# Token loads inside two attention projections, later waits at the cosine stage, and the context's high part behind the keys' in an eight-stage kernel

## The chip, the cores and the metric

The kernel runs on one core of one Trainium2 chip, as one program of 83187 instructions. The metric is the device time of one launch in microseconds (us). A core has five engines with queues of their own: PE (matrix products; its weight loads are listed as PEld), DVE (vector), ACT (scalar, activations), POOL (GpSimd) and SP, which here only issues transfers and waits. They order their work among each other by semaphores alone. A `Block` in the code holds one program for each engine and ends with a barrier of all of them.

## The reference, cut to what matters

Eight batches of 512 tokens of 256 numbers (4096 tokens, 4 MB) go through four layers. Each layer adds an attention over the context and then a feed-forward part:

```
x = x + attention0(context, layernorm(x), mask);     x = x + top-1 experts(layernorm(x))
x = x + cosine attention(layernorm(x), context);     x = x + expert choice(layernorm(x))
x = x + attention2(layernorm(x), context);           x = x + piecewise linear ffn(layernorm(x))
x = x + attention3(layernorm(x), context, mask);     x = x + top-2 experts(x)
```

Attentions 0, 2 and 3 have 16 heads of 16 numbers: `q = layernorm(x) Wq + bq`, `k = context Wk + bk`, `v = context Wv + bv`, softmax, and an output product. The cosine attention normalises tokens and context (with a gain `ln_g` and an offset `ln_b`), and needs sums over all tokens before it can weigh its three terms. Its weights are `w_in`, `w_out` and `b_out`.

## The kernel before, in words

The tokens are resident on the chip in `G.X`, 128 partitions x 32 tiles x 256 numbers. `build_program` fills constants in a first block, in which SP also stores a block of blank rows and loads the eight batches of tokens (L3312 to L3314, one semaphore `x_loaded[b]` for each). The eight stages follow one another, each of them blocks of its own.

**Projections** (`resident_projections`, L1353) are the first block of attentions 0, 2 and 3. Each product is made of three, from a high and a low part of both operands. Order by engine, for the batch b of the loop:

- SP loads the weights and the contexts of batches 0 and 1, five small tensors, for attention 0 also a mask; then in each round the context of b + 2 (it waits for `cT_low`), the stores of the key parts and of the query parts (four each), and what `prepare.loads` asks for: from round 4 on twelve loads of a group of heads (fourteen in attention 3), in attention 0 a mask of 1 MB in rounds 3 and 5.
- ACT: the root for the layernorm of b + 1 (`scalar_roots`), the high part of the context of b + 1 (`context_high`, L1460), the high part of the keys of b, of the queries of b (`high_part`, L1471), of the turned tokens of b + 1 (L230).
- POOL: the low part of the context of b (L1493), then what `prepare.gpsimd` asks for: in rounds 0 and 1 two fills each of `a_qs` or `a_ks` with ones (L1641); in attention 0 in rounds 2 to 7 conversions of the masks.
- DVE: the layernorm of b + 1 (statistics L200, aggregation L205, `a_p_var` L208, reciprocal L210, four `a_p_xn` L215), the low part of the keys of b (L1507), the values (L1528), the low part of the queries, of the turned tokens of b + 1 (L221).
- PE: keys, values, queries of b (24 products each, the 24 of the values half as wide), then eight transposes of `a_p_xn` of b + 1. Keys of b + 1 need the context's low part and free `psK` (`k_low`).

Key and query parts are held in one buffer in attention 0 and in two in the others. The profile writes `a_` for the prefixes of all three attentions.

**Cosine attention** (`cosine_attention`, L2046) first loads `win`, `wout` and `bout` in a block of their own with `load_weights` (L76), which waits until they have landed. `cosine_sums` (L2068) then loads `lng` and `lnb` the same way, sets two constants in a third block, and in a fourth goes over the batches: SP loads the context `cx`, DVE normalises, POOL applies gain and offset (L2177, L2178), PE turns and sums. `win` is first read in the next function, `wout` and `bout` in the one after.

**Expert choice** (`expert_choice`, L2700) uses the room of `G.X` for expert weights and keeps the tokens in DRAM (`x_dram`). At its end a block loads all 4 MB back and waits for them (L2711 to L2713). Attention 2 is the next stage.

Of the kernel before, what the change touches and what calls it, by code (L numbers as in the profile page):

```python
# [14 lines left out]
P = 128  # L15
B = 8
# [3 lines left out]
TB = S // P  # L20
# [1332 lines left out]
def resident_projections(nc, A, G, nm, w, q_scale, q_dram, k_dram, V, wo, bo, buffers, prepare):  # L1353

    with ExitStack() as ctx:
# [22 lines left out]
        rows = lambda x: x.rearrange("(k p) d -> p k d", p=P)  # L1378

        with nc.Block() as block:  # L1380
            @block.sync
            def _(sp):
                def context(b):
                    sp.dma_start(cT[:, b % 2], ctxT[:, :, b * S:(b + 1) * S]).then_inc(cT_loaded[b % 2], 16)

                sp.dma_start(raw["wk"][:], rows(w.Wk)).then_inc(w_loaded["wk"], 16)
                context(0)
                sp.dma_start(raw["wv"][:], rows(w.Wv)).then_inc(w_loaded["wv"], 16)
                sp.dma_start(raw["wq"][:], rows(w.Wq)).then_inc(w_loaded["wq"], 16)
                context(1)  # L1390
                smalls = ((bk[:], w.bk), (bv[:], bcast_row(w.bv)), (bq[:], w.bq), (wo[:], rows(w.Wo)), (bo[:], bcast_row(w.bo)))
                for tile, src in smalls:
# [10 lines left out]
                for b in range(B):  # L1403
                    if b + 2 < B:
                        sp.wait_ge(cT_low, b + 1)
                        context(b + 2)
                    sp.wait_ge(k_low, b + 1)
                    store(kp[:, b % buffers], k_dram[:, b], k_stored[b % buffers])
                    sp.wait_ge(q_low, b + 1)
                    store(qp[:, b % buffers], q_dram[:, b], q_stored[b % buffers])  # L1410
                    if b == 4:
                        for stored in k_stored + q_stored:
                            sp.wait_ge(stored, 64 * b // buffers)
                    prepare.loads(sp, b)
# [40 lines left out]
            def _(act):  # L1455
# [24 lines left out]
                for b in range(B):  # L1480
                    if b + 1 < B:
                        f.scalar_roots(act, b + 1)
                        context_high(b + 1)
                    high_part(k_in_psum, psK, kp, bk, k_stored, k_high, b)
                    high_part(q_in_psum, psQ, qp, bqs, q_stored, q_high, b)
                    if b + 1 < B:
                        f.scalar_high(act, b + 1, 0)
# [10 lines left out]
            def _(dve):  # L1498
# [11 lines left out]

                dve.wait_ge(G.x_loaded[0], 16)
                f.vector_norm(dve, 0, 0, first=True)
# [9 lines left out]
                for b in range(B):  # L1522
                    if b + 1 < B:
                        dve.wait_ge(G.x_loaded[b + 1], 16)
                        f.vector_norm(dve, b + 1, b + 1)
# [520 lines left out]
def cosine_attention(nc, A, G):  # L2046
# [4 lines left out]
    with ExitStack() as ctx:  # L2051
# [3 lines left out]
        bout = sb("bout", [P, D])  # L2055
# [3 lines left out]
        loaded = sem("loaded")  # L2059
        load_weights(nc, [(win[:], A["L1_xattn_w_in"].rearrange("(k p) o -> p k o", p=P)),  # L2060
                          (wout[:], A["L1_xattn_w_out"].rearrange("(h p) d -> p h d", p=P)),
                          (bout[:], bcast_row(A["L1_xattn_b_out"]))], loaded)
        cosine_sums(nc, A, G, z_dram, gsum)
        cosine_weights(nc, A, G, win, gsum, coef, wwh)
        cosine_apply(nc, A, G, z_dram, win, wout, bout, coef, wwh)


def cosine_sums(nc, A, G, z_dram, gsum):  # L2068


    with ExitStack() as ctx:
# [20 lines left out]
        zT_in_psum, zT_ready = [sem("zkT_in_psum"), sem("zqT_in_psum")], [sem("zkT_ready"), sem("zqT_ready")]  # L2092
        load_weights(nc, [(lng[:], bcast_row(A["L1_xattn_ln_g"])), (lnb[:], bcast_row(A["L1_xattn_ln_b"]))], loaded)
        with nc.Block() as block:
# [12 lines left out]
        with nc.Block() as block:  # L2107
            @block.sync
            def _(sp):
                load = lambda b, s: sp.dma_start(cx[:, s], ctx_rows[bass.ds(b, 1)].rearrange("a p t d -> p (a t) d")).then_inc(cx_loaded[s], 16)  # L2110
                load(0, 0)

                def step(b, u, i):
# [9 lines left out]
                for n in range(2):  # L2123
                    sp.wait_ge(z_stored[n], (B + 1) * 16)
                    sp.wait_ge(cx_loaded[n], (B // 2 + 1 - n) * 16)

            @block.tensor
# [41 lines left out]
            def _(pool):  # L2169
                def step(b, u, i):  # L2170
                    link = chained(pool, pool_chain, b * 2)

                    for z, x, ready, done in ((zk, nk, nk_ready, zk_ready), (zq, nq, nq_ready, zq_ready)):
# [4 lines left out]
                        nc.gpsimd.tensor_tensor(z[:, u], z[:, u], o, ALU.add).then_inc(done, 1)  # L2178

                rounds(pool, step)  # L2180

# [518 lines left out]
def expert_choice(nc, A, G):  # L2700
# [6 lines left out]
    with ExitStack() as ctx:  # L2707
        index = ctx.enter_context(nc.sbuf_tensor("l1f_index", [P, CE, SB], U32))
        choose_tokens(nc, A, G, sT_dram, index)
        run_experts(nc, A, G, rows_dram[0:N_TOK, :], x_dram, index)  # L2710
    with ExitStack() as ctx:  # L2711
        back = ctx.enter_context(stage_semaphores(nc, "l1f_"))("back")
        load_weights(nc, [(G.X[:], x_dram.rearrange("(n p) d -> p n d", p=P))], back)  # L2713

# [573 lines left out]
def build_program(nc, A, out, stages):  # L3288
    with ExitStack() as ctx:
# [11 lines left out]
        out_dram = out.rearrange("b s d -> (b s) d").rearrange("(n p) d -> p n d", p=P)  # L3301
        G.x_loaded, G.out = x_loaded, out_dram

        G.blank_rows = nc.dram_tensor("blank_rows", [P, TOP1_ROW], F32).ap()
        G.top1_rows = nc.dram_tensor("top1_rows", [TOP1_BLOCKS * P, TOP1_ROW], F32).ap()
        G.filled, blank_set, blank_stored = sem("filled"), sem("blank_set"), sem("blank_stored")
        with nc.sbuf_tensor("blank", [P, TOP1_ROW], F32) as blank, nc.Block() as block:
            @block.sync
            def _(sp):
                sp.wait_ge(blank_set, 2)  # L3310
                sp.dma_start(G.blank_rows, blank[:]).then_inc(blank_stored, 16)
                for b in range(B):  # L3312
                    sp.dma_start(G.X[:, b * TB:(b + 1) * TB, :], x_dram[:, b * TB:(b + 1) * TB, :]).then_inc(x_loaded[b], 16)
                sp.wait_ge(blank_stored, 16)  # L3314
# [58 lines left out]
```

## Time and profile before

| | us |
|---|---|
| median of three runs | 4579.55 (4572.97 to 4582.59) |
| the profiled execution, its own time | 4560.4 |
| its span | 4558.6 |
| PE busy | 3880.8 (85%) |
| DVE busy | 3103.2 (68%) |
| ACT busy | 2059.7 (45%) |
| POOL busy | 794.4 (17%) |

The span is what lies between the first and the last instruction of the profiled execution. Busy times are shares of that span; engines overlap, so that they don't add up. The span holds long stretches with different limits, and a mean over it says little of any one of them. Times in the rows below are counted from the span's start. Attention 0's projections lie between 10 and 137 us, the cosine attention begins at 1182, attention 2's projections lie between 2884 and 2996, attention 3's between 3743 and 3856.

### The profile page before, as it was taken

The numbers are of one execution on the slowest core, as the hardware profiler recorded it, in microseconds if no ns is written. First come the engines' busy times: TensorE is split into PE (matmuls) and PEld (weight loads), VectorE is DVE, ScalarE is ACT, GpSimd is POOL, SyncE is SP. The second block draws the span as 40 slices with busy tenths as digits, with TensorE's granted clock in tenths as the row PEclk, the third lists the DMA queues.
The fourth block names the chain that finished last, engine by engine and source line by source line (L and its number), as shares of the span: only waits on it lengthen the run. The fifth ranks groups of instructions, "written<-read, shape, count | busy, mean of one in ns | idle before, by whom it ended". The sixth has DMA issues, their size and how long they took to land. (4 is left out here: it accounts for less than half of the span.)

```text
span 4558.6 us, 83187 instructions
## 1 busy us (share of the span) xinstructions
PE 3880.8 (85%) x30525; PEld 2807.5 (62%) x30525; DVE 3103.2 (68%) x7110; ACT 2059.7 (45%) x3636; POOL 794.4 (17%) x510
## 2 busy tenths in 40 slices
PE   6699997799367999786389999579997987999899
PEld 5344444798265777676378888445555665455577
DVE  7666664446656666544556666678876888988688
ACT  3255554134013333243044444247775763777511
POOL 5424321401341000000023322310000003000000
PEclk9799998599678999898599999779998998999999
DMA  7333321201321000011054444532210005122000
GB/s 248 102 99 99 99 90 52 70 25 43 112 75 33 14 18 18 28 44 37 6 159 125 128 130 124 188 112 66 66 44 19 1 26 207 56 67 67 30 19 19
DMA packets 234365, 338.02 MB, mean 74 GB/s; under 512 B 39092, under 2 KB 132837, under 8 KB 234054
## 3 DMA queue, kind: packets, MB, share of 16 engines
q1 hardware_dynamic: 218168, 306.66, 21.1%
q0 software_dynamic: 15888, 27.23, 2.9%
q8 instruction: 195, 3.19, 0.3%
q14 instruction: 114, 0.93, 0.1%
HBM read 242.42 MB, written 107.01 MB: 77 GB/s over the span
## 5 line engine op out<-in xcount | busy, mean ns | idle before, releaser
L1905 ACT ACTIVATE a_pT<-a_psS 128x512 f32<-128x512 f32 x1536 | 835.9, 598 | 380.4 <-PE a_psS L1791 375.0
L1977 DVE TENSOR_REDUCE a_mx<-a_psA 128x1 f32<-128x512 f32 x1024 | 656.4, 685 | 77.4 <-PE a_psA L1769 77.4
L1806 PE MATMUL a_psZ<-a_pT,a_V 128*17 128x128 f32 x12288 | 485.8, 277 | 0.0
L1769 PE MATMUL a_psA<-a_ks,a_qs 48*128 48x512 f32 (+1 forms) x1536 | 402.8, 520 | 85.1 <-DVE a_mx L1977 36.8
L1973 DVE CUSTOM_DVE_ANT_0 a_scored<-a_psA,a_hide_q 128x512 bf16<-128x512 f32 x512 | 332.6, 688 | 182.1 <-PE a_psA L1769 181.0
L1806 PEld LDWEIGHTS a_psZ<-a_pT,a_V 128*17 128x17 f32 x12288 | 272.0, 97 | 269.4 <-issue 152.4
L1769 PEld LDWEIGHTS a_psA<-a_ks,a_qs 48*128 48x128 f32 (+1 forms) x1536 | 150.9, 191 | 331.4 <-DVE a_mx L1977 124.8
L1791 PE MATMUL a_psS<-a_qs,a_ks 50*128 50x512 f32 (+1 forms) x1536 | 316.3, 405 | 2.7 <-ACT a_pT L1905 0.8
L3245 DVE SCALAR_TENSOR_TENSOR ex_h<-ex_psU,ex_ub,ex_sg 128x512 f32<-128x512 f32 x129 | 96.9, 751 | 189.4 <-PE ex_psU L159 182.3
L1989 POOL TENSOR_TENSOR X<-X,a_osb 128x512 f32<-128x512 f32 x48 | 61.1, 1278 | 931.3 <-ACT a_osb L1892 913.3
L3191 ACT CAST ex_w_h<-X 128x1024 fp32r<-128x1024 f32 x102 | 106.0, 1040 | 151.0 <-DMA X<-in_L_ffn_gw 147.2
L1779 PE MATMUL a_psS<-a_hide_k,identb 128*128 128x512 bf16 x512 | 154.9, 384 | 16.5 <-ACT a_pT L1905 2.9
L3200 ACT ACTIVATE ex_sg<-ex_psG,ex_gb 128x512 f32<-128x512 f32 x129 | 88.8, 688 | 169.0 <-PE ex_psG L159 168.9
L3112 POOL DMA_INDIRECT ex_xg<-l1f_rows,ex_idx_get x72 | 75.4, 1047 | 511.5 <-DVEq L3276 361.8
L1791 PEld LDWEIGHTS a_psS<-a_qs,a_ks 50*128 50x128 f32 (+1 forms) x1536 | 148.5, 188 | 18.2 <-ACT a_pT L1905 13.1
L159 PE MATMUL ex_psY<-ex_w_h,ex_h_l 128*128 128x256 f32 x512 | 143.7, 281 | 0.0
L158 PE MATMUL ex_psY<-ex_w_l,ex_h_h 128*128 128x256 f32 x512 | 143.5, 280 | 0.0
L157 PE MATMUL ex_psY<-ex_w_h,ex_h_h 128*128 128x256 f32 x512 | 143.5, 280 | 0.0
L1148 PE MATMUL p_psY<-p_w,p_h 128*128 128x256 f32 x512 | 131.4, 392 | 13.5 <-ACT p_h L1225 13.5
L157 PE MATMUL l1a_psF<-l1a_win_h,l1a_zh 128*128 128x512 f32 x288 | 120.5, 418 | 25.4 <-DVE l1a_zl L2603 12.0
L1493 POOL TENSOR_TENSOR a_p_cT_l<-a_p_cT,a_p_cT_h 128x1024 fp32r<-128x1024 f32 x24 | 58.6, 2441 | 455.9 <-ACT a_p_cT_h L1460 455.4
L3205 ACT CAST ex_h_h<-ex_h 128x512 fp32r<-128x512 f32 x129 | 80.3, 623 | 116.7 <-DVE ex_h L3245 116.7
(606 smaller groups left out, 10221.8 us busy)
## 6 DMA issues: line engine op xcount, KB each, us to landing
a_qs<-a_q_parts SPq DMA_DIRECT2D x576, 64.0 KB, 2.3
a_ks<-a_k_parts SPq DMA_DIRECT2D x576, 64.0 KB, 2.3
a_k_parts<-a_p_kp SPq DMA_DIRECT2D x96, 256.0 KB, 2.6
a_q_parts<-a_p_qp SPq DMA_DIRECT2D x96, 256.0 KB, 3.1
X<-in_L_ffn_gw SPq DMA_DIRECT2D x36, 512.0 KB, 4.5
X<-in_L_ffn_up_w SPq DMA_DIRECT2D x36, 512.0 KB, 3.3
X<-in_L_ffn_down_w SPq DMA_DIRECT2D x36, 512.0 KB, 3.9
top_rows<-blank_rows SPq DMA_DIRECT2D x32, 514.0 KB, 5.0
```

The lines of the kernel that those rows point to most:

```text
L157: nc.tensor.matmul(out, wh, xh, start=start and n == 0, stop=False, **kw)
L158: nc.tensor.matmul(out, wh, xl, start=False, stop=False, **kw)
L159: last = nc.tensor.matmul(out, wl, xh, start=False, stop=stop and n == len(pairs) - 1, **kw)
L1148: last = nc.tensor.matmul(out, h[:, m % 2, t * P:(t + 1) * P], w2[:, m, :], start=False, stop=(m == MF - 1), skip_group_check=True)
L1769: nc.tensor.matmul(psA[:, unit(a, par) % 3], qs[r, g % ring, p % 2, q * P:(q + 1) * P], ks[r, g % ring, p % 2], start=True, stop=True).the ...
L1779: nc.tensor.matmul(psS[:, unit(t, par) % 3], G.identb[:], hide_k[:, u % 2, kt, :], start=True, stop=False, skip_group_check=True)
L1791: nc.tensor.matmul(psS[:, unit(t, par) % 3], ks[r, g % ring, p % 2, kt * P:(kt + 1) * P], qs[r, g % ring, p % 2], start=(hidden is None), ...
L1806: last = nc.tensor.matmul(psZ[q * VP:q * VP + VW, g % 2, j * P:(j + 1) * P], V[:, b, kt, g % NG * GH + j, :], pT[:, p % 2, par, kt, q * P: ...
L1905: nc.scalar.activation(pT[:, p % 2, par, kt, :], psS[:, unit(t, par) % 3], ACT.Exp).then_inc(exp_done, 1)
L1973: nc.vector.tensor_tensor_reduce(out=scored[:, par], in0=psA[:, unit(a, par) % 3], in1=hide_q[:, b % 2, q, :], scale=1.0, scalar=HIDDEN, o ...
L1977: nc.vector.tensor_reduce(mx[:, p // 2 % 2, par, p % 2, q:q + 1], psA[:, unit(a, par) % 3], AX_X, ALU.max).then_inc(a_used, 1)
L3191: nc.scalar.copy(w_h[:, s, c, :], whole[:, c, :]).then_inc(w_high, 1)
```

## The change

Four edits:

- The first block doesn't load the tokens any more. Attention 0's projections take them from `G.x_from`, batch by batch: batch 0 ahead of all weights, batch 1 after the context of batch 1, batch b + 2 at the head of round b.
- Expert choice doesn't load the tokens back. It leaves the place in DRAM in `G.x_from`, and attention 2's projections load them in the same way. `G.x_loads` counts the stages that did so, for the semaphore's value. Attention 3 has none to load.
- The cosine attention issues all five weight loads behind the load of the first context, in the block that goes over the batches. Only POOL waits for `lng` and `lnb`, ahead of its first round; SP waits for all of them at the block's end. Two blocks with waits are gone.
- In all three projections ACT makes the high part of the keys of b ahead of the high part of the context of b + 1.

```diff
@@ resident_projections
+        x_from, G.x_from = G.x_from, None
+        G.x_loads += x_from is not None
...
+                def tokens(b):
+                    if x_from is not None:
+                        tiles = slice(b * TB, (b + 1) * TB)
+                        sp.dma_start(G.X[:, tiles, :], x_from[:, tiles, :]).then_inc(G.x_loaded[b], 16)
...
+                tokens(0)
                 sp.dma_start(raw["wk"][:], rows(w.Wk)).then_inc(w_loaded["wk"], 16)
                 context(0)
                 sp.dma_start(raw["wv"][:], rows(w.Wv)).then_inc(w_loaded["wv"], 16)
                 sp.dma_start(raw["wq"][:], rows(w.Wq)).then_inc(w_loaded["wq"], 16)
                 context(1)
+                tokens(1)
...
                     if b + 2 < B:
+                        tokens(b + 2)
                         sp.wait_ge(cT_low, b + 1)
                         context(b + 2)
...
                         f.scalar_roots(act, b + 1)
+                    high_part(k_in_psum, psK, kp, bk, k_stored, k_high, b)
+                    if b + 1 < B:
                         context_high(b + 1)
-                    high_part(k_in_psum, psK, kp, bk, k_stored, k_high, b)
                     high_part(q_in_psum, psQ, qp, bqs, q_stored, q_high, b)
...
-                dve.wait_ge(G.x_loaded[0], 16)
+                dve.wait_ge(G.x_loaded[0], 16 * G.x_loads)
...
-                        dve.wait_ge(G.x_loaded[b + 1], 16)
+                        dve.wait_ge(G.x_loaded[b + 1], 16 * G.x_loads)
@@ cosine_attention
-        load_weights(nc, [(win[:], A["L1_xattn_w_in"].rearrange("(k p) o -> p k o", p=P)),
-                          (wout[:], A["L1_xattn_w_out"].rearrange("(h p) d -> p h d", p=P)),
-                          (bout[:], bcast_row(A["L1_xattn_b_out"]))], loaded)
-        cosine_sums(nc, A, G, z_dram, gsum)
+        loads = [(win[:], A["L1_xattn_w_in"].rearrange("(k p) o -> p k o", p=P)),
+                 (wout[:], A["L1_xattn_w_out"].rearrange("(h p) d -> p h d", p=P)),
+                 (bout[:], bcast_row(A["L1_xattn_b_out"]))]
+        cosine_sums(nc, A, G, z_dram, gsum, loads, loaded)
@@ cosine_sums
-        load_weights(nc, [(lng[:], bcast_row(A["L1_xattn_ln_g"])), (lnb[:], bcast_row(A["L1_xattn_ln_b"]))], loaded)
...
                 load(0, 0)
+                for tile, src in ((lng, "L1_xattn_ln_g"), (lnb, "L1_xattn_ln_b")):
+                    sp.dma_start(tile[:], bcast_row(A[src])).then_inc(loaded, 16)
+                for tile, src in later_loads:
+                    sp.dma_start(tile, src).then_inc(later_loaded, 16)
...
+                sp.wait_ge(loaded, 32)
+                sp.wait_ge(later_loaded, 16 * len(later_loads))
...
+                pool.wait_ge(loaded, 32)
                 rounds(pool, step)
@@ expert_choice
-    with ExitStack() as ctx:
-        back = ctx.enter_context(stage_semaphores(nc, "l1f_"))("back")
-        load_weights(nc, [(G.X[:], x_dram.rearrange("(n p) d -> p n d", p=P))], back)
+    G.x_from = x_dram.rearrange("(n p) d -> p n d", p=P)
@@ build_program
+        G.x_from, G.x_loads = x_dram, 0
...
-                for b in range(B):
-                    sp.dma_start(G.X[:, b * TB:(b + 1) * TB, :], x_dram[:, b * TB:(b + 1) * TB, :]).then_inc(x_loaded[b], 16)
```

## Rows read from the trace of the kernel before

**Rows 1.** Windows by stage: engines' busy us (count), granted clock, DMA share, GB/s.

```profile
10.00:23.00 13.00, 1.97 (x8) 1.53 (x8) 5.40 (x17) 5.12 (x7) 2.05 (x1) 1.00 1.09 361
...
1182.00:1197.00 15.00, 0.00 (x0) 0.00 (x0) 0.17 (x2) 0.00 (x0) 0.00 (x0) 0.50 0.55 166
...
2862.00:2884.00 22.00, 0.00 (x0) 0.00 (x0) 0.11 (x1) 0.15 (x1) 0.00 (x0) 0.50 0.64 197
...
2930.00:2941.00 11.00, 9.73 (x56) 8.20 (x56) 10.51 (x22) 4.67 (x9) 2.48 (x1) 1.00 0.67 240
```

**Rows 2.** Timeline, kernel's start: start us, us, engine, line, output<-input, count.

```profile
1.60 8.56 SPq L3313 DMA_DIRECT2D X<-in_x  x8
...
10.61 1.48 SPq L1386 DMA_DIRECT2D a_p_wk_raw<-in_L_xattn_Wk  x1
...
19.82 1.04 ACT L1460 CAST a_p_cT_h<-a_p_cT 128x1024 fp32r<-128x1024 f32 x1 [0.68 <-DMA a_p_cT<-in_ctxT]
```

**Rows 3.** DMA issues between 0 and 40 us: count, KB each, us to landing.

```profile
blank_rows<-blank SPq DMA_DIRECT2D x1, 128.5 KB, 3.3
```

**Rows 4.** Timeline, entry of the cosine attention.

```profile
1182.34 0.38 SPq L82 DMA_DIRECT2D l_win<-in_L_xattn_w_in  x1
...
1196.60 0.17 DVE L2097 MEMSET l1s_zeros<- 128x128 f32 x1 [16.63 <-PEq L78]
...
1197.25 1.19 SPq L2110 DMA_DIRECT2D l1s_cx<-in_ctx  x2
...
1201.20 1.41 DVE L2192 BATCH_NORM_STATS2 l1s_stats<-X 128x6 f32 x4 [4.43 <-DMA l1s_cx<-in_ctx]
```

**Rows 5.** Timeline, from the experts' end into attention 2, SP and ACT.

```profile
2869.03 0.39 SPq L82 DMA_DIRECT2D X<-l1f_x  x1
2883.84 0.39 SPq L1386 DMA_DIRECT2D a_p_wk_raw<-in_L_xattn_Wk  x1
...
2889.57 1.04 ACT L1460 CAST a_p_cT_h<-a_p_cT 128x1024 fp32r<-128x1024 f32 x1 [2.28 <-DMA a_p_cT<-in_ctxT]
```

**Rows 6.** DMA issues between 2920 and 2970 us.

```profile
a_p_cT<-in_ctxT SPq DMA_DIRECT2D x4, 512.0 KB, 4.3
```

**Rows 7.** Timeline of attention 2's round 2, by engine (ACT, POOL, DVE).

```profile
2925.59 0.21 ACT L226 ACTIVATE a_p_std<-a_p_var 128x4 f32<-128x4 f32 x1 [5.44 <-DVE a_p_var L208]
2925.70 1.03 ACT L1460 CAST a_p_cT_h<-a_p_cT 128x1024 fp32r<-128x1024 f32 x1
2926.64 1.26 ACT L1471 ACTIVATE a_p_kp<-a_p_psK,a_p_bk 128x512 fp32r<-128x512 f32 x2
...
2936.48 0.20 ACT L226 ACTIVATE a_p_std<-a_p_var 128x4 f32<-128x4 f32 x1 [5.44 <-DVE a_p_var L208]
...
2926.88 2.47 POOL L1493 TENSOR_TENSOR a_p_cT_l<-a_p_cT,a_p_cT_h 128x1024 fp32r<-128x1024 f32 x1 [8.42 <-ACT a_p_cT_h L1460]
...
2926.04 3.46 DVE L215 TENSOR_SCALAR a_p_xn<-X,a_p_meanvar,a_p_rstd 128x256 f32<-128x256 f32 x4
```

**Rows 8.** Timeline of DVE in attention 0 while POOL waits for a mask.

```profile
74.83 1.38 DVE L215 TENSOR_SCALAR a_p_xn<-X,a_p_meanvar,a_p_rstd 128x256 f32<-128x256 f32 x4
```

**Rows 9.** Timeline of POOL and DVE, attention 2's round 1; last row attention 0.

```profile
2905.81 8.82 POOL L1641 MEMSET a_ks<- 32x5120 f32 x2
...
2912.68 1.99 DVE L208 TENSOR_SCALAR a_p_var<-a_p_meanvar 128x4 f32<-128x4 f32 x1
...
85.25 10.44 DVE L215 TENSOR_SCALAR a_p_xn<-X,a_p_meanvar,a_p_rstd 128x256 f32<-128x256 f32 x4
```

**Rows 10.** Timeline of SP in attention 2 from the query store of round 4.

```profile
2955.08 2.45 SPq L1401 DMA_DIRECT2D a_q_parts<-a_p_qp  x4
...
2963.57 0.42 SPq L1384 DMA_DIRECT2D a_p_cT<-in_ctxT  x1
...
2989.06 2.68 SPq L1401 DMA_DIRECT2D a_q_parts<-a_p_qp  x4
```

**Rows 11.** Timeline of POOL in attention 0, the first conversion of the second mask.

```profile
79.37 5.38 POOL L1624 TENSOR_SCALAR a_is_hidden<-a_m_int 128x2048 f32<-128x2048 int32 x1 [12.12 <-DMA a_m_int<-in_maskT]
```

More of the change, by code:

```diff
@@ L2059, in cosine_attention, with cosine_sums @@
         loaded = sem("loaded")
-        load_weights(nc, [(win[:], A["L1_xattn_w_in"].rearrange("(k p) o -> p k o", p=P)),
-                          (wout[:], A["L1_xattn_w_out"].rearrange("(h p) d -> p h d", p=P)),
-                          (bout[:], bcast_row(A["L1_xattn_b_out"]))], loaded)
-        cosine_sums(nc, A, G, z_dram, gsum)
+        loads = [(win[:], A["L1_xattn_w_in"].rearrange("(k p) o -> p k o", p=P)),
+                 (wout[:], A["L1_xattn_w_out"].rearrange("(h p) d -> p h d", p=P)),
+                 (bout[:], bcast_row(A["L1_xattn_b_out"]))]
+        cosine_sums(nc, A, G, z_dram, gsum, loads, loaded)
         cosine_weights(nc, A, G, win, gsum, coef, wwh)
         cosine_apply(nc, A, G, z_dram, win, wout, bout, coef, wwh)
-def cosine_sums(nc, A, G, z_dram, gsum):
+def cosine_sums(nc, A, G, z_dram, gsum, later_loads, later_loaded):
     with ExitStack() as ctx:
```

## The prediction

> **What bounds the kernel now.** I read the page's 40 slices first: PE is busy over most of the span, but not everywhere, so a mean can't price this change. Next came windows on the five places it touches. In two of them all engines stand still and only transfers run: 15 us at the cosine attention's entry, 22 us between the experts and attention 2 [rows 1]. Last I read timelines. They show what ends those pauses [rows 4, 5], what ends the wait at the kernel's start [rows 2], and which engine sets a round of the projections. In an undisturbed round of attention 2 the roots stand 2936.48 - 2925.59 = 10.9 us apart [rows 7]; DVE is busy for 10.51 of 11 us, PE for 9.73, ACT for 4.67 [rows 1]. DVE sets the round, and PE's 9.7 is the next floor.
>
> **Part 1, tokens at the kernel's start.** SP spends 8.56 us on issuing eight token loads, and the weights follow at 10.61; the first context's high part, from which the keys follow, starts at 19.82 because its transfer is late [rows 2]. That is 9.2 us after the stage's first load. The same way takes 2889.57 - 2883.84 = 5.7 us in attention 2, with an empty queue [rows 5]. After the change the first block ends once the blank rows have landed: issued just ahead of the token loads, at about 1.2, plus 3.3 [rows 3], plus 0.45 for the barrier (wk follows the last token issue, 1.60 + 8.56 = 10.16, by that much) = 4.95. One token batch (512 KB) now stands ahead of weights and context. At the 361 GB/s that the queue moves while it is full [rows 1] it takes 1.4 us. So the high part starts at 4.95 + 5.7 + 1.4 = 12.05, 7.8 earlier. I take 7.5, with 5 (slow first issues, 1.07 us each in the row of eight) and 8.5 as ends. The layernorm of batch 0 isn't later: tokens landed after some 3.5 us plus 2.2 of statistics come to 5.7, before the context's 7.1.
>
> **Part 2, cosine entry.** Two blocks of loads go. DVE's constants, at 1196.60, move to where SP issued the first load, 1182.34, and the context load follows 0.65 us behind as now (1197.25): at 1183.0, 14.25 earlier [rows 4]. The context needs 3.95 us to land now (1201.20), with one context behind it. Five loads, 2.4 MB, now queue behind it; I allow 0.45 for packets that mix. Sum 13.8, ends 12 and 14.3. Hidden: POOL first needs gain and offset some 7 us after DVE's first statistics, that is 11 us after the issue, and the second context (behind all five, about 9 us) is needed 14 us after the first. If that cover were gone, POOL would start late by the difference, once.
>
> **Part 3, entry of attention 2.** SP's load of all tokens is issued at 2869.03, the stage's first load at 2883.84 [rows 5]. The block between them goes: 14.8 us. The context of batch 0 stands behind one token batch: 1.4 us back. Gain 13.4, ends 10 and 14.8 (nothing given back).
>
> **Part 4, six token loads in the rounds.** In a round SP issues 0.45 us more and the queue moves 0.5 MB more beside 2.6 MB; its share goes from 0.67 [rows 1] to some 0.8. SP waits for DVE there, so the issue is free. The load for batch b + 2 starts behind the query store of b - 1, some 2.3 us after DVE has made it, and DVE reads it 1.1 us plus a round after it: 9.7 + 1.1 - 2.3 = 8.5 us of cover. A context, the same size from the same place in the queue, lands in 4.3 [rows 6]; with 1.4 for the tokens that is 5.7. In rounds 4 to 6 of attention 2 SP issues without a gap from 2955.08 to 2989.06 + 2.68 = 2991.74, and the stage ends behind that. There the load for batch 7 (beside the context at 2963.57) costs its 0.45 [rows 10]. It may also land up to 3 us after DVE wants it, which is hidden: DVE's last results wait for SP then.
>
> **Part 5, the order on ACT.** Four `a_p_xn` take 3.46 us while POOL makes the context's low part (2926.88 to 2929.35), and end when it ends [rows 7]; the same four take 1.38 while POOL is idle [rows 8]. DVE loses 2.08 us a round by this overlap. With the keys' high part first (two instructions, 1.15 us until the next can start) POOL starts about 2.4 us after the root instead of 1.3, and the four end 1.8 after it: no overlap. The keys' high part needs nothing that is late: the root comes some 2 us after the keys' last product. DVE alone would then need 8.8 us a round, PE needs 9.7, and the context's low part, 1.15 later, ends 4.9 us after the root, just when PE wants it. So a round becomes 9.7, a gain of 1.2.
>
> The Trainium skill ("SBUF — State Buffer", on engine ports) says that VectorE's two-port operations and GpSimd share one port pair as an exclusive lock for a whole instruction, first come first served. By that rule four xn cost either 1.38 or what POOL leaves, never a mixture; rows 7 and 8 agree. The rule also speaks against this change where POOL's work is long, which is priced next from rows.
>
> Where POOL has more to do, the shift costs. In round 1 of attentions 2 and 3 it fills a stack with two instructions, 8.82 us [rows 9]. DVE's `a_p_var` waited there to their end (2912.68 + 1.99), and in attention 0 four xn took 10.44 us while POOL ran three instructions back to back, so one DVE instruction gets in between two of POOL's [rows 9]. After the change the fills stand at 2907.0 to 2911.4 to 2915.8. DVE is there 2.1 earlier (2910.6), passes at 2911.4, and its first xn waits until 2915.8, the second behind the context's low part until 2918.3. The keys' low part starts at 2919.0 against 2918.5: 0.4 lost. The next rounds give back 1.9 (DVE has slack over PE there), then 0.4, then 1.2 and a last 0.5 at the query part that SP stores at 2955.08: 3.6 us in each stage. From there SP's issues set the end, so rounds 5 to 7 bring nothing. Attention 3: 3.6. Attention 2: 3.6 - 0.45 = 3.1. Ends for each: -1 (all rounds like round 1) and 7 (1.2 in six rounds).
>
> In attention 0 POOL has 7 us of fills or mask work in rounds 0 to 3, and the root waits for it: up to 1.15 us a round lost, 3.5 in all. But POOL then waits 12.12 us for a mask [rows 11] that SP issues behind the queries of round 3. These come 0.8 to 3 us earlier by my walk through the rounds, depending on whether DVE slips between two fills. I take 1.0, ends -3.5 and 3.
>
> **Sum.** 7.5 + 13.8 + 13.4 + 1.0 + 3.1 + 3.6 = 42.4 us. The profiled execution, 4560.4 (span 4558.6), would become 4518.0. It lies 19 us under the median of the runs shown; against that median, 4579.55, the forecast is **4537 us**.
>
> **Rivals.**
> - *The order on ACT pays back less than it costs*: in each round with POOL work the chain root, keys' high, context's high, low part, POOL's own work grows by 1.15 us, and that chain sets the round: three rounds of attention 0 and two each of attentions 2 and 3, 8 us lost and the 7.7 of part 5 not won. 42.4 - 7.7 - 8 = 27 us gained: 4553. For it: `a_p_var` ends with POOL's fill [rows 9]. Against: undisturbed rounds are set by DVE.
> - *The order pays fully*, 1.2 us in six rounds of each of attentions 2 and 3 and 3 us in attention 0: 34.7 + 3 + 6.7 + 7.2 = 52 gained: 4528. Against: SP's gapless issues from round 4.
> - *The entries were hidden anyway*: the blocks' waits go, but the first context lands as late because the queue is as full. All load bytes still stand in one queue. Then parts 1 to 3 bring half, 17 us, 25 in all: 4555. Against: only one token batch is ahead of what PE needs.
> - *Slower*: token loads arrive late in every round, and DVE, which takes them in order, waits with all behind it (keys' low part, stores, PE). They have 8.5 us of cover. Each us above it costs 12 us (six rounds, two stages); the gain of 42 is gone from 8.5 + 3.5 = 12 us to landing. At 14 us it is +24: 4604. Against: 4.3 for a context in that place [rows 6].
>
> **How the numbers follow.** The forecast with its own ends holds 0.62, the order's loss 0.13, its full pay 0.12, half-hidden entries 0.07, late tokens 0.03 (a part of which ends within the bound), the rest mishaps and the scatter of runs, whose three span 10 us. Range 4519 to 4557: from both good ends (60 gained) down to 22 gained. This kernel's measurement tells some 0.2%, 9 us, from no change. Faster by more: 0.95; within: 0.03; slower: 0.02.
>
> **What would show it.** The high part of context 0 starts near 12 us after the span's start; the cosine context load less than 1 us after the end of the top-1 stage's barrier, with DVE's statistics 4 to 4.5 us behind; the pause before attention 2 shrinks by 13; four xn take 1.4 in rounds 2 to 6, with rounds of 9.7 us in attentions 2 and 3; round 1 longer. Waits of DVE's statistics for X in the rounds, or POOL ahead of the root in them, would prove me wrong. If the DVE stall stays at 2 us a round though POOL starts later, part 5 is wrong.

## The result and the profile after

The changed kernel took 4534.9 us in the median of four runs (4525.88 to 4540.46), the kernel before 4576.69 beside it (4572.97 to 4582.59, four runs). The ratio is 0.9908, 95% interval 0.9892 to 0.9924: 42 us faster. A later set gave 4539.0 (six runs) beside 4574.09, ratio 0.9919, 0.9906 to 0.9932. Forecast: 4537, range 4519 to 4557; it was counted down from 4579.55, the median of the three runs known then. The profiled execution took 4525.88 us.

The page of the changed kernel, first lines:

```profile
span 4524.1 us, 83053 instructions
...
PE 3878.7 (86%) x30431; PEld 2817.1 (62%) x30525; DVE 3076.4 (68%) x7110; ACT 2058.1 (45%) x3636; POOL 794.6 (18%) x510
```

PE's work is as before (3880.8 us). DVE's busy time fell by 27 us with the same work. The `a_p_xn` of all three projections together take 57.8 us, where they took 85.6: what went are stalls that the profile counts as busy. The kernel's start, changed kernel, timeline:

```profile
4.27 0.45 SPq L1390 DMA_DIRECT2D X<-in_x  x1
4.77 0.50 SPq L1396 DMA_DIRECT2D a_p_wk_raw<-in_L_xattn_Wk  x1
...
8.53 1.41 DVE L200 BATCH_NORM_STATS2 a_p_stats<-X 128x6 f32<-128x256 f32 x4 [8.53 <-DMA X<-in_x]
...
11.33 1.03 ACT L1472 CAST a_p_cT_h<-a_p_cT 128x1024 fp32r<-128x1024 f32 x1
```

The stage's first load is issued at 4.27, and the first high part starts at 11.33, not at 19.82 [rows 2]. The entry of the cosine attention, changed kernel, timeline:

```profile
1170.40 1.23 DVE L1044 TENSOR_TENSOR X<-X,m_rows 128x1024 f32<-128x1024 f32 x1 [0.23 <-DMA m_rows<-m_z]
1174.07 0.17 DVE L2109 MEMSET l1s_zeros<- 128x128 f32 x1 [2.44 <-PEq L46]
...
1174.74 0.38 SPq L2122 DMA_DIRECT2D l1s_cx<-in_ctx  x1
1175.17 0.50 SPq L2125 DMA_DIRECT2D l1s_lng<-in_L_xattn_ln_g  x1
...
1178.83 1.41 DVE L2211 BATCH_NORM_STATS2 l1s_stats<-X 128x6 f32 x4 [4.59 <-SPq L2131]
```

Between the barrier and the context's load no other load is waited for, and the statistics come 4.1 us after its issue, nearly as before (3.95) [rows 4]. POOL's first product with the gain comes 7.08 us after the first statistics in both kernels, so POOL doesn't wait for `lng` and `lnb`. The releaser of the last row is given as a wait of SP; the time is that of the load's landing. The entry of attention 2, changed kernel, SP and ACT:

```profile
2848.11 0.39 SPq L1390 DMA_DIRECT2D X<-l1f_x  x1
2848.56 0.50 SPq L1396 DMA_DIRECT2D a_p_wk_raw<-in_L_xattn_Wk  x1
...
2854.83 1.03 ACT L1472 CAST a_p_cT_h<-a_p_cT 128x1024 fp32r<-128x1024 f32 x1
```

The high part starts 6.7 us after the first load of the tokens, where it was 2889.57 - 2869.03 = 20.5 [rows 5]. Rounds 1 and 2 of attention 2, changed kernel, timelines of ACT, POOL and DVE:

```profile
2876.42 0.65 DVE L208 TENSOR_SCALAR a_p_var<-a_p_meanvar 128x4 f32<-128x4 f32 x1
2877.57 7.15 DVE L215 TENSOR_SCALAR a_p_xn<-X,a_p_meanvar,a_p_rstd 128x256 f32<-128x256 f32 x4
...
2892.49 1.38 DVE L215 TENSOR_SCALAR a_p_xn<-X,a_p_meanvar,a_p_rstd 128x256 f32<-128x256 f32 x4
...
2872.69 8.79 POOL L1654 MEMSET a_ks<- 32x5120 f32 x2
2881.55 2.37 POOL L1506 TENSOR_TENSOR a_p_cT_l<-a_p_cT,a_p_cT_h 128x1024 fp32r<-128x1024 f32 x1
2894.47 2.40 POOL L1506 TENSOR_TENSOR a_p_cT_l<-a_p_cT,a_p_cT_h 128x1024 fp32r<-128x1024 f32 x1 [10.55 <-ACT a_p_cT_h L1472]
...
2892.03 0.20 ACT L226 ACTIVATE a_p_std<-a_p_var 128x4 f32<-128x4 f32 x1 [5.77 <-DVE a_p_var L208]
2901.76 0.20 ACT L226 ACTIVATE a_p_std<-a_p_var 128x4 f32<-128x4 f32 x1 [3.34 <-DVE a_p_var L208]
```

In round 2 the four `a_p_xn` end at 2893.87, before POOL starts at 2894.47: 1.38 us, not 3.46 [rows 7]. In round 1 they stand behind the fill and the low part for 7.15 us: the first takes 4.06 (to the fill's end), the second 2.53 (to the low part's end), the last two 0.40 each. Windows over one undisturbed round of attention 2 and one of attention 3, changed kernel (columns as in [rows 1]):

```profile
2892.03:2901.76 9.73, 9.73 (x62) 8.56 (x61) 8.50 (x20) 4.47 (x8) 2.40 (x1) 1.00 0.88 311
3767.20:3777.00 9.80, 9.80 (x62) 8.71 (x61) 8.51 (x20) 4.47 (x7) 2.40 (x1) 1.00 0.79 285
```

PE is busy all of the round: it has taken DVE's place as what sets it. SP's tail of attention 2 and, last, DVE's wait for the tokens of batch 7, changed kernel:

```profile
2917.53 2.75 SPq L1412 DMA_DIRECT2D a_q_parts<-a_p_qp  x4
...
2926.00 0.43 SPq L1390 DMA_DIRECT2D X<-l1f_x  x1
...
2929.55 3.61 SPq L1412 DMA_DIRECT2D a_q_parts<-a_p_qp  x4
...
2952.62 2.79 SPq L1412 DMA_DIRECT2D a_q_parts<-a_p_qp  x4
...
2930.40 1.41 DVE L200 BATCH_NORM_STATS2 a_p_stats<-X 128x6 f32<-128x256 f32 x4 [2.25 <-DMA X<-l1f_x]
```

From the query store of round 4 to the end of the last it is 37.9 us, and 36.7 before (2991.74 - 2955.08) [rows 10]: 0.47 of the token load, the rest slower issues. Attention 0, POOL of the changed kernel:

```profile
70.53 5.38 POOL L1637 TENSOR_SCALAR a_is_hidden<-a_m_int 128x2048 f32<-128x2048 int32 x1 [9.64 <-DMA a_m_int<-in_maskT]
...
100.60 7.09 POOL L1622 TENSOR_SCALAR a_hide_q<-a_m_int 128x2048 bf16<-128x2048 int32 x1 [12.01 <-DMA a_m_int<-in_mask_Bx1xSxS_ik]
```

The wait that was 12.12 us [rows 11] is now 9.64 and ends 8.84 us earlier, about as much as the stage started earlier (8.49). SP's queue shows why, first in the kernel before, then in the changed kernel:

```profile
71.20 1.82 SPq L1401 DMA_DIRECT2D a_q_parts<-a_p_qp  x4
73.06 0.45 SPq L1603 DMA_DIRECT2D a_m_int<-in_maskT  x1
```

```profile
62.37 1.80 SPq L1412 DMA_DIRECT2D a_q_parts<-a_p_qp  x4
64.21 0.46 SPq L1616 DMA_DIRECT2D a_m_int<-in_maskT  x1
```

Counted from the first high part, the queries of round 3 are stored at 51.0 us, where it was 51.4, and the mask's conversion follows its issue by 6.3 us in both. Nothing of the new order came through. The statistics of batch 2 come 1.5 us earlier than before (17.9 for 19.5), those of batch 4 come 0.5 later (42.0 for 41.5), because the two rounds between them take 12.0 us each for 11.0. POOL reached its wait 2.1 us later than before.

### The profile page after: what moved, and what is told of

The parts are those of the page before. It is cut to its first block and busy times, and to the rows that moved or that the text cites. A ratio compares the mean times of both kernels' runs of the same rounds, so it can differ in the third digit from the quotient of the medians.

```text
span 4524.1 us, 83053 instructions
## 1 busy us (share of the span) xinstructions
PE 3878.7 (86%) x30431; PEld 2817.1 (62%) x30525; DVE 3076.4 (68%) x7110; ACT 2058.1 (45%) x3636; POOL 794.6 (18%) x510
## 5 line engine op out<-in xcount | busy, mean ns | idle before, releaser
L1792 PE MATMUL a_psS<-a_hide_k,identb 128*128 128x512 bf16 x418 | 133.8, 383 | 28.0 <-ACT a_pT L1918 15.8
```

The source lines that it names most:

```text
L1792: nc.tensor.matmul(psS[:, unit(t, par) % 3], G.identb[:], hide_k[:, u % 2, kt, :], start=True, stop=False, skip_group_check=True)
```

## The experiments

The table takes the touched stretches alone, from each kernel's profile, in us. *start*: the first context's high part, from the span's start. *a0*: first context's high part to the end of attention 0's projections (DVE's `memset` of `a_nparts`). *cos*: end of the last addition before the cosine attention to its first statistics. *entry*: from the start of DVE's last group on `ex_y` (the experts' result) to attention 2's first high part. *a2*: from there to the query store of round 4, and to the end of the projections. *a3*: first statistics to the same two places. *sh*: the shared expert (part of expert choice), from first to last of its normalizing instructions, whose code no kernel changes.

| kernel | start | a0 | cos | entry | a2 | a3 | sh |
|---|---|---|---|---|---|---|---|
| before | 19.82 | 117.68 | 21.24 | 36.38 | 65.51, 106.95 | 71.41, 113.24 | 196.5 |
| changed | 11.33 | 117.63 | 7.20 | 22.58 | 62.70, 105.11 | 66.58, 109.23 | 196.9 |
| changed, again | 10.75 | 119.45 | 7.10 | 23.07 | 62.34, 104.59 | 66.62, 108.27 | 207.4 |
| old order | 11.06 | 119.16 | 7.27 | 22.90 | 66.10, 109.22 | 69.90, 111.64 | 207.6 |
| cosine only | 19.79 | 122.38 | 7.09 | 35.11 | 65.89, 106.78 | 71.67, 113.81 | 207.5 |
| tokens only | 12.14 | 123.04 | 21.04 | 22.71 | 66.04, 108.27 | 71.84, 114.24 | 196.3 |
| order only | 20.01 | 119.29 | 20.69 | 34.94 | 63.41, 105.55 | 66.89, 109.25 | 196.5 |
| masks earlier | 10.94 | 106.52 | 7.09 | 22.67 | 62.84, 105.78 | 66.54, 108.22 | 200.4 |
| fills spread | 11.00 | 120.27 | 7.11 | 22.71 | 55.24, 97.48 | 59.06, 101.54 | 196.5 |
| both | 10.95 | 107.71 | 7.10 | 22.66 | 55.27, 97.53 | 58.93, 101.78 | 196.3 |
| both, again | 11.55 | 106.09 | 7.08 | 22.59 | 55.24, 97.85 | 59.68, 102.12 | 196.9 |
| tokens first | 22.27 | 119.39 | 7.20 | 32.79 | 62.27, 103.00 | 66.95, 109.19 | 196.6 |
| a round later | 10.72 | 142.80 | 7.05 | 22.60 | 81.07, 140.06 | 67.07, 108.59 | 207.5 |

The runs were made in four sets, not all on one chip, each with the kernel before beside it: its medians are 4576.69, 4573.53, 4572.0 and 4574.09. So where two kernels come from different sets, their distance is also given "by the ratios": the difference of their ratios to the kernel before, times 4574 us. The changed kernel has two ratios, 0.9908 and 0.9919, which gives two ends.

**The change without its new order.** Edit to the changed kernel:

```diff
                         f.scalar_roots(act, b + 1)
+                        context_high(b + 1)
                     high_part(k_in_psum, psK, kp, bk, k_stored, k_high, b)
-                    if b + 1 < B:
-                        context_high(b + 1)
```

> The changed kernel with the old order on ACT (context's high part ahead of the keys'). Theory: the order brought 2 to 3 us in attention 2 and 4 in attention 3 by taking four xn out of POOL's way, and nothing in attention 0, where masks set the end; so this kernel takes 5 to 8 us more than the changed one and about 35 less than the one before. Its xn are 3.46 us again in rounds 2 to 6 and its rounds 10.9 us. Rival (the order costs as much as it brings): same time as the changed kernel within 2 us. Rival (the order is most of the gain): 15 us or more above the changed kernel.

4545.22 us (4532.69 to 4552.47), ratio 0.9939 (0.9916 to 0.9963). The old order costs 109.22 - 105.11 = 4.1 us in attention 2 and 2.4 in attention 3, together within the 5 to 8 expected. The median is 10.3 us above the changed kernel's 4534.9, and 9 to 14 by the ratios; what lies beyond the two stretches isn't explained. Its timeline of DVE in attention 2 has the old stall in rounds 2 and 3, though all else is new:

```profile
2903.23 3.45 DVE L215 TENSOR_SCALAR a_p_xn<-X,a_p_meanvar,a_p_rstd 128x256 f32<-128x256 f32 x4
...
2914.11 3.46 DVE L215 TENSOR_SCALAR a_p_xn<-X,a_p_meanvar,a_p_rstd 128x256 f32<-128x256 f32 x4
```

**Each part alone**, put into the kernel before: the cosine hunks, the token hunks (the block of the start and that of expert choice together), the order.

```diff
# cosine only
-        cosine_sums(nc, A, G, z_dram, gsum)
+        cosine_sums(nc, A, G, z_dram, gsum, loads, loaded)
# tokens only
-        load_weights(nc, [(G.X[:], x_dram.rearrange("(n p) d -> p n d", p=P))], back)
+    G.x_from = x_dram.rearrange("(n p) d -> p n d", p=P)
# order only
+                    high_part(k_in_psum, psK, kp, bk, k_stored, k_high, b)
+                    if b + 1 < B:
                         context_high(b + 1)
-                    high_part(k_in_psum, psK, kp, bk, k_stored, k_high, b)
```

> The kernel before with the cosine attention's loads alone changed. Theory: the stage's first statistics start 14 us earlier and all of it reaches the end: 14 us under the kernel before. Rival (the weights are still waited for later): the gain is under 5 us, and a pause shows ahead of the sums' end or the next function.

> The kernel before with the token loads alone changed, old order on ACT, old cosine entry. Theory: 8.5 us at attention 0's first context and 13.8 at attention 2's, less 0.5 at attention 2's end for the issue of batch 7: 21 to 22 us under the kernel before. In this order a round takes 10.9 us, so batch 7's tokens land less late than in the changed kernel (under 1 us of wait for X). Rival (loads late in every round): DVE waits for X in several rounds and the gain falls under 15.

> The kernel before with the order on ACT alone changed. Theory: attention 0's projections end within 1 us of before; attention 2's end 3 to 4 us earlier relative to their start (no token load stands in SP's gapless issues), attention 3's 4; together 7 us under the kernel before. In round 1 of both, four xn take 7 us. Rival (port contention is not what lengthens xn): xn stay at 3.4 us in rounds 2 to 6 although POOL starts later. Rival (the order loses where POOL has work): slower than before.

Cosine only: 4563.26 (4554.62 to 4570.93, ten runs), ratio 0.9977 (0.9962 to 0.9991). Tokens only: 4550.06 (4547.15 to 4554.33), 0.9958 (0.9942 to 0.9975). Order only: 4568.48 (4559.93 to 4575.96, ten runs), 0.9995 (0.9986 to 1.0005), whose interval holds 1; its stretches tell it from nothing: 1.4 us in attention 2, 4.0 in attention 3. Against the 4573.53 of the kernel before in that set the medians are 10.3, 23.5 and 5.1 lower (14, 21 to 22 and 7 were expected), 38.9 in all; by the ratios they are 10.5, 19.2 and 2.3, 32.0 in all; the whole change brought 42 and 35. The touched stretches say it best: 14.1 at the cosine entry, 7.7 + 13.7 at the two entries, 1.4 + 4.0 in the rounds, 40.9 beside 42.2 for the whole. So within the scatter the parts add up, and nothing shows that one needs another. Attention 0's rest was 5.4 us longer with the tokens alone and 4.7 longer with the cosine hunks alone, which don't touch it: differences of 5 us in that stretch can't be read. With the tokens alone DVE waited 3.27 us for the late `a_bo`, and 0.66 in the kernel before.

The profiled execution of cosine only was 9.2 us longer than that of the kernel before, though its cosine entry is 14.1 us shorter. The stretch *sh* shows where part of that went: cosine only was 10.9 us ahead at its start and 0.1 behind at its end. Another 9 us were lost after it. Windows over it in cosine only, then in the changed kernel:

```profile
1915.80:2123.30 207.50, 179.31 (x983) 156.02 (x984) 86.86 (x188) 84.43 (x117) 0.00 (x0) 0.87 0.13 40
```

```profile
1905.20:2102.10 196.90, 173.43 (x982) 148.59 (x983) 86.85 (x189) 84.40 (x117) 0.00 (x0) 0.92 0.14 43
```

DVE and ACT do the same work in both; PE has the same count of instructions at a mean granted clock of 0.87, not 0.92, and is busy for 6 us more of the 10.6. Four of the thirteen profiled executions of the table (changed again, old order, cosine only, a round later) took some 207.5 us there at 0.86 or 0.87, eight some 196.5 at 0.92, and one 200.4 at 0.90. The changed kernel shows both.

**Masks a round earlier.** Edit to the changed kernel:

```diff
-            if hidden is not None and b in (3, 5):
-                load_mask(sp, (b - 1) // 2)
+            if hidden is not None and b in (2, 4):
+                load_mask(sp, b // 2)
```

> The changed kernel, with the two later masks of attention 0 issued one round earlier (in rounds 2 and 4, not 3 and 5). Theory (attention 0's middle rounds wait for masks, so the new order could bring nothing there): POOL's two waits of 9.6 and 12.0 us for a mask shrink below 2 us each and the stage's end, at 128.96 us in the changed kernel, comes 8 to 14 us earlier; the median is 8 to 14 us under the changed kernel's 4534.9, so 4521 to 4527. Rival (the mask's 4 us issue-side place is taken from the stores, or DVE's own work sets these rounds): the waits go but the end moves by under 3 us, median 4532 to 4538.

4516.87 (4516.02 to 4517.74), ratio 0.9878 (0.9862 to 0.9895). Attention 0's projections are 117.63 - 106.52 = 11.1 us shorter, inside the 8 to 14 expected. The median is 18.0 us under the changed kernel's 4534.9, and 14 to 19 by the ratios, so somewhat more than the stretch explains. Its timelines have one wait of POOL for a mask left, and a new one of DVE, for the tokens of batch 7:

```profile
85.70 7.09 POOL L1622 TENSOR_SCALAR a_hide_q<-a_m_int 128x2048 bf16<-128x2048 int32 x1 [2.27 <-DMA a_m_int<-in_mask_Bx1xSxS_ik]
...
89.60 1.41 DVE L200 BATCH_NORM_STATS2 a_p_stats<-X 128x6 f32<-128x256 f32 x4 [4.26 <-DMA X<-in_x]
```

The masks' landing had set those rounds. With it out of the way the late token load of the last batch is what shows next (3.2 and 4.4 us in the two profiles of *both*).

**Fills spread.** Edit to the changed kernel, for attentions 2 and 3:

```diff
-            if b < 2:
+            if hidden is None and b < 4:
+                half = (32, 96)[b % 2]
+                nc.gpsimd.memset((qs, ks)[b // 2][half:half + 32].bitcast(F32), 1.0).then_inc(stacks_set, 1)
+                pool.wait_ge(stacks_set, b + 1)
+            if hidden is not None and b < 2:
```

> The changed kernel, with the four fills of POOL in attentions 2 and 3 spread one per round over rounds 0 to 3, where they were two in each of rounds 0 and 1. Theory (one DVE instruction slips between two of POOL's, the rest wait for the engine's whole stretch; the order loses in round 1 because a fill and the low part lie back to back beside the four normalizing instructions): in round 1 the slow instruction (7.15 us) goes back to under 3.5 us, and the part up to the query store of round 4 is 4 to 7 us shorter in each of the two stages; median 8 to 14 us under the changed kernel's, 4521 to 4527. Rival (POOL's fill time is on the chain anyway, so that spreading moves the loss to rounds 2 and 3): each of the four rounds loses 4.4 us of POOL in the chain root, fill, low part, and the stages' ends stay within 1.5 us; median 4532 to 4538.

4523.59 (4513.41 to 4526.2), ratio 0.9887 (0.987 to 0.9905). The part up to the query store of round 4 is 7.5 us shorter in both stages (62.70 to 55.24, 66.58 to 59.06), over the 4 to 7 expected; the median is 11.3 us under the changed kernel's, and 10 to 15 by the ratios. Timelines of POOL and DVE in attention 2's round 1, fills spread:

```profile
2872.08 2.40 POOL L1506 TENSOR_TENSOR a_p_cT_l<-a_p_cT,a_p_cT_h 128x1024 fp32r<-128x1024 f32 x1 [4.75 <-ACT a_p_cT_h L1472]
2874.53 4.37 POOL L1654 MEMSET a_qs<- 32x5120 f32 x1
...
2870.08 1.38 DVE L215 TENSOR_SCALAR a_p_xn<-X,a_p_meanvar,a_p_rstd 128x256 f32<-128x256 f32 x4
```

The fill ends at 2878.90, just before DVE's next `a_p_var` at 2879.07, so neither waits for the other; the `a_p_xn` take 1.38 or 1.39 in every round of attention 2, and no stall of DVE on a fill is left there.

**Both.** The two edits together, in two sets of runs.

> Both at once: masks one round earlier in attention 0, fills spread in attentions 2 and 3. By the theories of the two single runs they act in different stages and add up: 16 to 28 us under the changed kernel's median, 4507 to 4519. By the rivals: under 4 us, 4531 to 4539. If only one of the two holds: 4521 to 4527.

> The kernel with the masks of attention 0 one round earlier and the fills of attentions 2 and 3 spread over four rounds, run again in more rounds beside the kernel before. Its first run gave 4500.0. Theory (both edits add up): 4500 +- 8, ratio to the kernel before 0.982 to 0.987. Rival (part of the 35 us below the changed kernel was the scatter of one set of runs): 4512 to 4520, ratio 0.987 to 0.989.

> The changed kernel itself, beside the two others of this set, so that both differences are read on one chip and in one set of runs. Theory: 4535 +- 8, ratio to the kernel before 0.989 to 0.993; stages' steps as in its first profile within 1 us where PE's clock has no part (first context's high part, the cosine attention's statistics, attention 2's first context). Rival (the steps hold by chance): any of these three off by more than 2 us.

First set 4500.04 (4495.18 to 4512.13), ratio to the kernel before 0.9848 (0.9827 to 0.9868); second 4509.07 (4503.24 to 4511.14), 0.9856 (0.9839 to 0.9873), beside the changed kernel's 4539.0 in the same set. That is 30 us below the changed kernel and beats both single edits. The second median lies 1 us outside the expected 4500 +- 8, its ratio inside; the two medians stand 9 us apart. The stretches of the first profile add up to 25: 9.9 in attention 0, 7.4 in attention 2 and 7.7 in attention 3 (up to the query store of round 4). A window over a later round of attention 2, both edits:

```profile
2879.84:2889.59 9.75, 9.75 (x62) 8.58 (x61) 8.50 (x20) 4.46 (x8) 2.41 (x1) 1.00 0.96 337
```

PE stays the floor of the round. The changed kernel, run again, had start, cosine entry and attention 2's entry within 0.6 us of its first profile, as expected.

**Tokens first.** Edit to the changed kernel: all eight batches ahead of the weights, in both stages, still inside the stage's block.

```diff
-                tokens(0)
+                for b in range(B):
+                    tokens(b)
                 sp.dma_start(raw["wk"][:], rows(w.Wk)).then_inc(w_loaded["wk"], 16)
```

> The changed kernel, but all eight token batches issued ahead of the first weight load in both stages (still inside the stage's block, so the separate blocks' waits stay gone). Theory (what was won at the two entries is the queue's order: weights and context no longer behind 4 MB of tokens): the context's high part comes 7 batches x 1.4 us = 9.8 us later than in the changed kernel in attention 0 (at 21.1) and in attention 2, so nearly all of the entries' gain but the last microseconds goes; median 18 to 22 us above the changed kernel's, 4553 to 4557. Rival (the gain was the block's wait, that is the landing and the barrier of a separate load): the context comes 7 x 0.45 = 3.2 us later, for the issues alone, and the median is 5 to 8 us above, 4540 to 4543.

4547.39 (4535.31 to 4555.27), ratio 0.9951 (0.9935 to 0.9968). The first high part is 10.9 us later than in the changed kernel in attention 0 and 10.2 in attention 2, for 9.8 expected. Its timelines of SP and ACT at attention 2's entry:

```profile
2850.81 7.42 SPq L1390 DMA_DIRECT2D X<-l1f_x  x8
2858.26 1.42 SPq L1397 DMA_DIRECT2D a_p_wk_raw<-in_L_xattn_Wk  x1
...
2866.24 0.63 ACT L1475 ACTIVATE a_p_wk_h<-a_p_wk_raw 128x512 fp32r<-128x512 f32 x1 [9.14 <-DMA a_p_wk_raw<-in_L_xattn_Wk]
2867.60 1.04 ACT L1471 CAST a_p_cT_h<-a_p_cT 128x1024 fp32r<-128x1024 f32 x1 [0.73 <-DMA a_p_cT<-in_ctxT]
```

In attention 2 most of the entry's 13.8 us hung on what is ahead in the queue, and 3.6 on the block's wait itself (2.2 if the 35 us of the other two old entries are taken). At the kernel's start all 8.5 hung on the queue: the high part comes at 22.27, 2.4 us later than in the kernel before. The rival's 3.2 us are refuted, but not because issues cost nothing: in a row of eight an issue takes 0.93 us, not 0.45, so SP reaches `wk` 7.45 us after its first token load, where it took 0.45. That is 7.0 of the 10 us; 3 more come on the way from there to the high part. Whether the issues are slow because the queue is full, no run separates. Against the 4534.9 of the first set the median moved by 12.5 us, by the ratios by 15 to 20, for 18 to 22 expected. In the profiled execution the unchanged code between attention 0's projections and the first statistics of the cosine attention took 1039.7 us, where the other kernels with the new cosine entry took 1046.7 to 1052.3; why isn't settled.

**Tokens a round later.** Edit to the changed kernel:

```diff
                 context(1)
-                tokens(1)
...
+                    if b + 1 < B:
+                        tokens(b + 1)
                     if b + 2 < B:
-                        tokens(b + 2)
```

> The changed kernel, but each token batch of attentions 0 and 2 is issued one round later (in round b the load of b + 1, not b + 2), so that the cover of a whole round is gone. Theory (the prediction's slower case): the load is issued 2.3 us after DVE's last result of the round before and lands 4.3 to 5.7 us later, DVE wants it 1.1 us after that result and stands still with everything behind it, so each round is 5.5 to 6.9 us longer, six or seven rounds in each of two stages, less some 8 us that SP's gapless tail of attention 2 had anyway: 60 to 80 us above the changed kernel, 4595 to 4615, above the kernel before. Rival (the batches' 4 MB share the queue so well, or PE and SP have so much slack beside DVE, that a late batch costs little): rounds under 12 us, less than 25 us in all, median under 4560.

4591.01 (4589.18 to 4604.89) beside 4574.09, ratio 1.0037 (1.0024 to 1.0051): slower than the kernel before. DVE in attention 2, tokens a round later, timeline:

```profile
2921.81 1.41 DVE L200 BATCH_NORM_STATS2 a_p_stats<-X 128x6 f32<-128x256 f32 x4 [7.79 <-DMA X<-l1f_x]
...
2937.05 1.41 DVE L200 BATCH_NORM_STATS2 a_p_stats<-X 128x6 f32<-128x256 f32 x4 [6.34 <-DMA X<-l1f_x]
...
2952.67 1.41 DVE L200 BATCH_NORM_STATS2 a_p_stats<-X 128x6 f32<-128x256 f32 x4 [6.38 <-DMA X<-l1f_x]
...
2967.57 1.41 DVE L200 BATCH_NORM_STATS2 a_p_stats<-X 128x6 f32<-128x256 f32 x4 [6.00 <-DMA X<-l1f_x]
...
2988.36 1.40 DVE L200 BATCH_NORM_STATS2 a_p_stats<-X 128x6 f32<-128x256 f32 x4 [11.89 <-DMA X<-l1f_x]
...
3008.24 1.40 DVE L200 BATCH_NORM_STATS2 a_p_stats<-X 128x6 f32<-128x256 f32 x4 [10.99 <-DMA X<-l1f_x]
```

Three rounds are 15 to 16 us long, the last two 21 and 20. Attention 0's projections grew by 25.2 us and attention 2's by 35.0, 60 in all, the low end of the 60 to 80 expected; the median moved by 52 to 56, under it. So the change lives on issuing each batch a round ahead.

## Why the prediction was right

- **Part 1, the start.** Predicted 7.5 us with 5 and 8.5 as ends, measured 8.49, the upper end; 9.1 in the second profile, over it, and 7.7 with the tokens alone. The blank rows landed after 2.7 us where 3.3 was taken, so the stage's first issue came at 4.27, not at 4.95; from there to the high part it was 7.06, against 5.7 + 1.4 = 7.1. The price of one batch in the queue was right: seven batches cost 10.9 and 10.2 us in *tokens first*, 1.5 each for 1.4. In that run 7.0 of the 10 us are longer issues on SP; whether the bytes behind them are the reason is open.
- **Part 2, the cosine entry.** 13.8 predicted, 14.04 measured, 14.1 with the cosine hunks alone. The loads behind the context cost it 0.14 us (4.09 to the statistics against 3.95), not 0.45. The cover for gain and offset was there: POOL starts at the same 7.08 us.
- **Part 3, attention 2's entry.** 13.4 predicted, 13.8 measured; 13.3 again, 13.7 with the tokens alone. But without the tokens' edit this stretch also took 34.94 and 35.11 in two kernels (36.38 before), so some 1 us of it is scatter and the gain may be 12.4.
- **Part 4, tokens in the rounds.** Right. Behind the first batch no statistics wait for tokens in the changed kernel's attention 0, nor in rounds 1 to 5 of attention 2; there batch 7 came 2.25 us late, for up to 3 foreseen, and was hidden behind SP's tail. With the cover gone DVE waited 6 to 8 us in four rounds of attention 2 and 11 to 12 in the last two: the mechanism of the rival of late tokens is real, and only the cover kept it away.
- **Part 5, the order in attentions 2 and 3.** The mechanism holds: four `a_p_xn` take 1.38, the rounds 9.73 and 9.36. Two of its terms were mis-sized. Round 1 lost more: from the first high part to the root of round 2 it is 36.02 us before (2925.59 - 2889.57) and 37.20 now, 1.2 lost for 0.4 [rows 5, 7]. The walk let the first `a_p_xn` wait for the second fill and the second for the low part, and so it went, for 7.15 us; it added up to a smaller loss than was measured. The rounds behind it gave 29.49 - 25.50 = 4.0, the 4.0 of the walk (1.9 + 0.4 + 1.2 + 0.5). SP's tail then gave back 1.2 us where 0.45 was foreseen. So attention 2 brought 1.84, not 3.1; attention 3 brought 4.83 up to the query store, 4.0 at the end, for 3.6.
- **Part 5 in attention 0.** 1.0 predicted, 0.05 measured. The step that failed was that the queries of round 3, and the mask behind them, come 0.8 to 3 us earlier: counted from the first high part they came 0.3 us earlier (51.0 for 51.4). The loss foreseen for the early rounds came in two of them, 1 us each, and POOL's wait for the mask absorbed it. That the masks set these rounds is shown by *masks earlier*. A gain of 1 us can't be read in the whole stretch: the same code took 117.68 in one profile and 122.38 in another.
- **The sum.** 8.49 + 14.04 + 13.80 + 0.05 + 1.84 + 4.01 = 42.2 in the touched stretches for 42.4 predicted. That it is this close is luck in part: parts 1 to 3 brought 1.6 us more than predicted, part 5 brought 1.8 less. The span fell by 34.5 only: the untouched last stages had lost 5.6 us between attention 3 and the end in that execution (40.08 ahead at attention 3's end). The medians stand 42 and 35 apart in the two sets; the forecast of 4537 lies between 4534.9 and 4539.0, closer than that scatter lets it claim.
- **The rivals.** The order alone neither lost 8 us nor paid fully (*order only*: 5.4 us in its stretches). The entries were not hidden: in the changed kernel's profile the stretches behind them shrank or stayed within 1 us of before. Loads that were late in every round came only when they were issued a round later.

## What to carry to other kernels

A block that only loads and waits has two costs. One is its landing and barrier: 14 us for the two blocks at the cosine entry. The other is that its loads stand ahead of the first operands of the next stage: 10 of the 13.8 us at attention 2's entry. Put one piece ahead and issue the rest a full round before its use, and price that cover: one round less turned 35 to 42 us gained into 17 lost. Where two engines exclude each other, move the work by one short instruction to where the other is idle, and spread long fills one to a round: spreading the same fills won 7.5 us per stage. When an improvement in a round brings nothing, look for a transfer that is issued a fixed number of rounds ahead; it may set the pace, as the masks did in attention 0.

## What the runs showed of the hardware

- Four normalizing instructions take 1.38 us, 3.46 beside one POOL instruction of 2.4 us, and 7.15 beside a fill and a low part. Timed against POOL, the first waits to the end of a POOL instruction, gets in, and the next waits for the one behind it. This is what the Trainium skill says of the port pair of the two engines ("SBUF — State Buffer", on engine ports): an exclusive lock for a whole instruction. The trace agrees, and shows that a POOL instruction that only writes (the fill) blocks DVE too.
- PE's mean granted clock in unchanged code differs from one execution to the next: 0.92 in eight profiles of the shared expert (196.5 us), 0.86 or 0.87 in four (207.5 us), 0.90 in one (200.4 us). A single profile can't show a gain of 10 us in the span; the length of a touched stretch can.
- The issue of a token load on SP took 0.39 to 0.65 us in the changed kernel, but for one of 1.53, and 0.93 or 1.07 in a row of eight (7.42 and 8.57 us in *tokens first*). A row of loads also delays what is behind it by SP's time.
